# Cross-attention with layer norm: attention values in two halves per block, and a new written order of the steps on every engine

## The chip, the cores and the metric

One core of a Trainium2 chip runs the whole program. The metric is the device time of one execution in microseconds (us). Engines are called by the profile's names: PE (matmul; PEld its weight loads), DVE (vector), ACT (scalar activation), POOL (GpSimd), SP (issues the DMAs).

## The reference

Four batches of 2048 rows of `x` (512 wide) attend to 77 context rows each, with 16 heads of 32. The result passes the output projection, is added to `x` and normalised:

```python
qh = split(x @ Wq.T + bq); kh = split(ctx @ Wk.T + bk); vh = split(ctx @ Wv.T + bv)
scores = einsum('bhqd,bhkd->bhqk', qh, kh) / sqrt(32);  masked where mask == 0
e = exp(scores - max(scores)) * mask;  probs = e / (sum(e) + 1e-9)
out = einsum('bhqk,bhkd->bhqd', probs, vh) @ Wo.T + bo + x
y = (out - mean(out)) / sqrt(var(out) + 1e-5) * ln_g + ln_b
```

All arrays are float32. The kernel keeps most of that accuracy by splitting operands in a high and a low part and making three products of each.

## The kernel before

The 8192 rows of `x` are taken in 16 blocks `b` of 512 rows, four blocks to a batch. For each block the steps are:

- `Q(b, g)`: 12 matmuls of 512 columns, four times (g is a group of four heads). Before it ACT writes the high part of `xT` (`XT_hi`, two halves), POOL the low part (`XT_lo`). ACT and DVE then take the result out of the bank (`Q_hi`, `Q_lo`).
- `S(b, t, half)`: scores of 128 rows `t` and eight heads, 6 matmuls of 308 columns, eight times. DVE adds the mask bias (`bias`) and takes the maximum (`row_max`); ACT makes eight exponentials (`exponent`); after `add_eps` and `inverse`, POOL multiplies (`normalise`) and DVE transposes into TP (`turn`). There is one pair of score banks, so each `S` waits until `bias` has emptied it.
- `AV(b)`: probabilities times values, on 32x32 tiles of the array, a loop over four head groups g. It begins when all four `turn` of the block are done. `AT_hi_` (ACT) and `AT_lo_` (DVE) take it out.
- `OUT(b, i)`: 12 matmuls of 512 columns, four times. DVE runs `residual`, `stats`, `aggregate`, `center` on the bank. Then come `inv_std` (POOL), `LN_scale` (ACT), `add_beta` (POOL) and the store (SP).

`Q` and `OUT` share two PSUM banks, `qo_bank`. `QO_TURN` (L174) lists the eight units of a step, and a unit takes bank 0 or 1 by its place in this list. `qo_free` waits until the unit two places ahead has been emptied.

Nothing is scheduled at run time. Each engine has its own order written out by hand, one software-pipelined loop over steps `s` (PE L115, ACT L213, DVE L673, POOL L769, SP L295), and each instruction waits on semaphores. A step of PE holds S of block s-1, Q of block s, and AV and OUT of block s-2. PE runs, in a step, `AV(s - 2)` whole between `S(s - 1, 1, 1)` and `Q(s, 0)` (L121).

Ahead of the loop come the keys (`K`) and in its first steps the values (`V`) of all four batches. Both go through DRAM: SP stores `V_st` to V_scratch once per batch (L287), and `load_V` (L254) brings a batch back in 24 DMAs in the layout of AV; `load_K` (L240) does it for keys in 4. `V_add` (L571) on DVE writes `V_st`, which has two buffers, so the fourth waits until the second is stored. SP's order before the loop is: load_K(0), xT(1), rows(0), the V stores with load_V(0) after the first, load_K(1), load_V(1). xT(2) and all later loads come behind this.

The program text of PE reaches it by an instruction queue, q8 in the profile. Both its weight loads and its matmuls are instructions.

Of the kernel before, what the change touches and what calls it, by code (L numbers as in the profile page):

```python
# [40 lines left out]
def xattn_program(nc, xT, x, ctxT, mask, WqT, WkT, WvT, WoT, qk_b, bv, bo, ln_g, ln_b, out):  # L41
# [6 lines left out]
    with es:  # L48
# [127 lines left out]
        QO_SLOT = {(kind, i): (n, lag) for n, (kind, i, lag) in enumerate(QO_TURN)}  # L176
        assert len(QO_SLOT) == 2 * T

        def qo(kind, i):
            return qo_bank[QO_SLOT[kind, i][0] % 2]  # L180

        def qo_before(kind, b, i):
            n, lag = QO_SLOT[kind, i]
            s = b + lag
            while s >= -1:
                s, n = (s, n - 2) if n >= 2 else (s - 1, n + 2 * T - 2)
                other, j, lag = QO_TURN[n]
                if has(s - lag):
                    return other, s - lag, j
            return None  # L190
# [618 lines left out]
```

## Time and profile before

| | |
|---|---|
| median of 3 runs | 795.63 us (794.51 to 800.0) |
| profiled execution: its time | 795.72 us |
| its span, first to last instruction | 793.9 us |
| PE busy | 646.9 us (81%) |
| DVE / ACT / POOL busy | 530.6 / 529.2 / 429.7 us |
| mean granted TensorE clock | 0.872 of full |
| first AV starts / last AV starts / last instruction ends | 117.0 / 754.4 / 793.9 us |

Read it by stages: up to the first AV (117 us) is the prologue. From the second AV (158.6 us) to the fifteenth (715.6 us) the loop repeats. After that the pipeline drains. Busy shares are averages over all three. In the view of groups a matmul of full float32 counts as two instructions: an AV of one block has 192 in the program's order and 384 in the trace, with as many weight loads.

### The profile page before, as it was taken

Reading aid. Unit: us, or ns where it says so; the run is one execution under the profiler, and the core shown is the slowest. Engines: PE = TensorE matmul, PEld = TensorE weight load, DVE = VectorE, ACT = ScalarE, POOL = GpSimd, SP = SyncE. Lnnn points to the kernel's source line nnn. Section 1 sums busy time; section 2 is a strip of 40 time slices with the busy share of each in tenths; the row PEclk is TensorE's granted clock in tenths of the full one; section 3 lists DMA queues with packets and bytes.
Section 4 is the critical chain, followed back from the end, with each engine's and each line's share of the span. In section 5 each row is a group of like instructions: output and inputs, shape, how many; then the busy total and the mean of one; then the engine's idle time right before and its main releaser. Section 6 shows DMA issues by size and latency. Waiting matters only on the chain.

```text
span 793.9 us, 21417 instructions
## 1 busy us (share of the span) xinstructions
PE 646.9 (81%) x8544; PEld 529.6 (67%) x8544; DVE 530.6 (67%) x798; ACT 529.2 (67%) x2362; POOL 429.7 (54%) x332
## 2 busy tenths in 40 slices
PE   4694068989898979799898989897979899897664
PEld 4573057767676868677776767685868677676553
DVE  5445064959595967769594959586877859596733
ACT  6253275859594968669594959495968859586521
POOL 4401143557657573837574665757483747555553
PEclk9798558989897989989897989798998979896977
DMA  9703210302222031404140232203140402020202
GB/s 319 243 8 65 92 53 2 113 23 83 81 79 84 19 131 29 147 15 148 45 138 26 81 97 63 99 8 142 47 148 14 147 15 93 16 81 29 80 30 79
DMA packets 36549, 63.80 MB, mean 80 GB/s; under 512 B 12660, under 2 KB 15124, under 8 KB 34273
## 3 DMA queue, kind: packets, MB, share of 16 engines
q1 hardware_dynamic: 36304, 62.42, 24.0%
q8 instruction: 67, 1.10, 0.5%
q14 instruction: 34, 0.27, 0.1%
q10 hardware_dynamic: 144, 0.00, 0.0%
HBM read 43.43 MB, written 18.67 MB: 78 GB/s over the span
## 4 chain that ended last, share of the span: by engine, by line
PE 66%; DVE 16%; issue 10%; SPq 3%; DMA 2%; ACT 1%; POOL 1%; POOLq 0%; DVEq 0%
PE qo_bank L313 39%; PE av_bank L398 14%; PE s_bank L313 11%; DVE E L589 3%; DVE TP L617 3%; DVE qo_bank L633 3%; SPq L254 2%; DVE bn L639 2%; PE av_bank L313 2%; DVE neg_max L598 2%; DVE AT_lo L625 1%; DMA V_scratch<-V_st 1%; DMA xT_raw<-in_xT 1%; POOL xT_lo L730 1%; DMA qk_bias<-in_qk_b 1%
## 5 line engine op out<-in xcount | busy, mean ns | idle before, releaser
L482 ACT ACTIVATE E<-E,neg_max 128x77 f32<-128x77 f32 x1024 | 352.2, 350 | 15.8 <-DVE neg_max L598 15.8
L749 POOL TENSOR_TENSOR E<-E,inv_sum 128x1232 f32<-128x1232 f32 x64 | 145.7, 2277 | 209.8 <-DVE inv_sum L606 209.8
L482 ACT ACTIVATION_READ_ACCUMULATOR E<-E,neg_max 128x1 f32 x1024 | 194.6, 190 | 0.0
L398 PE MATMUL av_bank<-TP,Vp 32*32 32x128 f32 x6144 | 109.0, 326 | 52.5 <-issue 49.7
L398 PEld LDWEIGHTS av_bank<-TP,Vp 32*32 32x32 f32 x6144 | 84.8, 114 | 73.0 <-issue 63.2
L313 PE MATMUL qo_bank<-xT_hi,WqT_lo 128*128 128x512 f32 x256 | 85.3, 462 | 42.5 <-DVE QT_lo L577 35.2
L625 DVE TENSOR_TENSOR AT_lo<-av_bank,AT_hi 128x512 fp32r<-128x512 f32 x64 | 43.0, 675 | 112.9 <-ACT AT_hi L497 112.9
L589 DVE TENSOR_TENSOR E<-s_bank,mask_bias 128x616 f32<-128x616 f32 x128 | 101.0, 789 | 25.9 <-PE s_bank L313 22.8
L497 ACT ACTIVATE AT_hi<-av_bank 128x512 fp32r<-128x512 f32 x64 | 36.0, 592 | 119.7 <-PE av_bank L398 119.7
L767 POOL TENSOR_TENSOR Y<-Y,b_row 128x512 f32<-128x512 f32 x64 | 82.7, 1294 | 60.1 <-ACT Y L505 60.1
L313 PE MATMUL s_bank<-Kd,QT_hi 128*128 128x308 f32 x512 | 114.1, 310 | 0.0
L313 PE MATMUL s_bank<-Kd,QT_lo 128*128 128x308 f32 x256 | 81.8, 320 | 26.9 <-DVE E L589 24.7
L730 POOL TENSOR_TENSOR xT_lo<-xT_raw,xT_hi 128x1024 fp32r<-128x1024 f32 x32 | 77.4, 2422 | 46.0 <-ACT xT_hi L461 46.0
L598 DVE TENSOR_REDUCE neg_max<-E 128x8 f32<-128x624 f32 x128 | 100.0, 781 | 1.2
L617 DVE STREAM_TRANSPOSE TP<-E 128x1280 f32<-128x1280 f32 x64 | 95.6, 1494 | 1.0 <-POOL E L749 1.0
L577 DVE SCALAR_TENSOR_TENSOR QT_lo<-qo_bank,qk_bias,QT_hi 128x512 fp32r<-128x512 f32 x64 | 47.5, 742 | 70.9 <-ACT QT_hi L473 70.9
L313 PEld LDWEIGHTS qo_bank<-xT_hi,WqT_lo 128*128 128x128 f32 x256 | 53.0, 220 | 57.3 <-DVE QT_lo L577 35.8
L313 PEld LDWEIGHTS s_bank<-Kd,QT_hi 128*128 128x128 f32 x512 | 87.1, 194 | 4.8
L473 ACT ACTIVATE QT_hi<-qo_bank,qk_bias 128x512 fp32r<-128x512 f32 x64 | 43.7, 682 | 68.3 <-PE qo_bank L313 68.3
L313 PE MATMUL qo_bank<-WoT_lo,AT_hi 128*128 128x512 f32 x256 | 74.2, 414 | 9.7 <-DVE Y L653 8.1
L313 PE MATMUL qo_bank<-xT_lo,WqT_hi 128*128 128x512 f32 x256 | 81.7, 447 | 0.0
L741 POOL TENSOR_TENSOR Y<-Y,bo_row 128x1024 f32<-128x1024 f32 x32 | 74.6, 2353 | 3.4 <-DMA Y<-in_x 3.3
(65 smaller groups left out, 934.0 us busy)
## 6 DMA issues: line engine op xcount, KB each, us to landing
xT_raw<-in_xT SPq DMA_DIRECT2D x16, 1024.0 KB, 5.9
Y<-in_x SPq DMA_DIRECT2D x16, 1024.0 KB, 5.6
out_y<-Y SPq DMA_DIRECT2D x64, 256.0 KB, 3.7
Vp<-V_scratch SPq DMA_DIRECT2D x48, 32.0 KB
K_scratch<-TP SPq DMA_DIRECT2D x1, 1232.0 KB, 9.2
E<-in_WkT SPq DMA_DIRECT2D x4, 256.0 KB, 5.5
Y<-in_WqT SPq DMA_DIRECT2D x4, 256.0 KB, 6.6
TP<-in_WvT SPq DMA_DIRECT2D x4, 256.0 KB, 9.7
```

The lines of the kernel that those rows point to most:

```text
L313: last = mm(bank, a, b, start=(n == 0), stop=(n == len(products) - 1))
L398: last = mm(av_bank[DK * j:DK * j + DK, q, g * P:g * P + P], Vp[part, b // BB % 2, par, kb, u, :], TP[part, 5 * u + 2 * par + kb, :, :].re ...
L482: last = cp(e, e, ACT.Exp, bias=neg_max[:, t, h:h + 1], accum_out=rowsum[:, t, h:h + 1])
L577: stt(out=QT_lo[:, b % 2, g, :], in0=qo("Q", g)[:, :], scalar=qk_bias[:, g:g + 1], in1=QT_hi[:, b % 2, g, :].bitcast(FP32), op0=ALU.add, o ...
L589: tt(E[:, t, 8 * half:8 * half + 8, 0:SK].rearrange("p (g j) k -> p g j k", g=2), s_bank[:, :, 0:GK].rearrange("p g (j k) -> p g j k", j=H ...
L598: nc.vector.tensor_reduce(out=neg_max[:, t, 8 * half:8 * half + 8], in_=E[:, t, 8 * half:8 * half + 8, 0:SK + 1], op=ALU.max, axis=AX.X, n ...
L617: nc.vector.transpose(TP[:, :, t, :], E[:, t, :, :].rearrange("p h k -> p (h k)") .rearrange("p (n q) -> p n q", q=Q32)).then_inc(t_ready, 1)
L625: tt(AT_lo[:, :, cols], av_bank[:, i, :].rearrange("p (g r) -> p g r", g=C), AT_hi[:, :, cols].bitcast(FP32), ALU.subtract).then_inc(at_lo, 1)
L730: nc.gpsimd.tensor_tensor(out=xT_lo[:, b % 2, cs, :], in0=xT_raw[:, b % 2, cs, :], in1=xT_hi[:, b % 2, cs, :].bitcast(FP32), op=ALU.subtra ...
L741: nc.gpsimd.tensor_tensor(out=y, in0=y, in1=bo_row[:, :].unsqueeze(1).broadcast_to((P, 2, D)), op=ALU.add).then_inc(x_bo_ready, 1)
L749: nc.gpsimd.tensor_tensor(out=e, in0=e, in1=inv_sum[:, t, :].unsqueeze(2).broadcast_to((P, H, SK)), op=ALU.mult).then_inc(probs_ready, 1)
L767: nc.gpsimd.tensor_tensor(out=y, in0=y, in1=b_row[:, :], op=ALU.add).then_inc(normed, 1)
```

## The change

The arithmetic is the same, and so is the number of instructions of each kind on PE. What changes is order and place:

- `AV(b, pair)` has two parts, of two head groups (eight heads) each. In a step, PE now has `AV(s-2, 0)`, `S(s-1, 1, 1)`, `Q(s, 0)`, `S(s-1, 2, 0)`, `AV(s-2, 1)`. Its end is signalled after the second part only.
- `QO_ORDER` lists all 128 units of `Q` and `OUT` for the whole program, with other lists for the first and last steps, and gives each its bank in alternation. `OUT(b, 2)` and `OUT(b, 3)` stand together at the head of the next step.
- Each engine's loop has its own lists for the first and last steps. ACT takes AT_hi of all four parts together. Stores of a block go out together.
- In the prologue: the low part of the first xT is made by DVE (`XT_lo_first`) and not by POOL. The high parts of that xT come before those of the keys. `ctxT_hi/lo` lie in the second half of Kd (so this is zeroed later, in `zero_Kd_1`). load_K(1) and load_V(1) move behind xT(2) to xT(5) and rows(1), rows(2). Projections of block 0 start before the values.

```diff
-        QO_TURN = (("OUT", 3, 3), ("Q", 0, 0), ("Q", 1, 0), ("OUT", 0, 2),
-                   ("Q", 2, 0), ("OUT", 1, 2), ("Q", 3, 0), ("OUT", 2, 2))
+        QO_TURN = (("OUT", 3, 2), ("OUT", 3, 3), ("Q", 0, 0), ("Q", 0, 1), ("OUT", 2, 0), ("Q", 0, 2), ("OUT", 2, 1), ("Q", 0, 3))
...
+                    19: (("OUT", 15, 0), ("OUT", 15, 1), ("OUT", 15, 2), ("OUT", 15, 3),)}
...
+        def qo(kind, b, i):
+            return qo_bank[QO_PLACE[kind, b, i] % 2]
...
+                if b in (2, BB + 1, 2 * BB + 1):
+                    load_K(b // BB + 1)
+                    load_V(b // BB + 1)
...
-            load_K(1)
-            load_V(1)
...
-            def AV(b):
+            def AV(b, pair):
...
-                for g in range(C):
+                for g in (2 * pair, 2 * pair + 1):
...
-                last.then_inc(av_ps, 1)
+                if pair == 1:
+                    last.then_inc(av_ps, 1)
...
-                OUT(s - 3, 3), S(s - 1, 1, 1), AV(s - 2), Q(s, 0), S(s - 1, 2, 0), Q(s, 1), S(s - 1, 2, 1)
-                OUT(s - 2, 0), S(s - 1, 3, 0), Q(s, 2), S(s - 1, 3, 1), OUT(s - 2, 1)
+                    OUT(s - 3, 2), OUT(s - 3, 3), S(s - 1, 0, 1), S(s - 1, 1, 0), AV(s - 2, 0)
+                    S(s - 1, 1, 1), Q(s, 0), S(s - 1, 2, 0), AV(s - 2, 1), Q(s, 1)
+                    S(s - 1, 2, 1), OUT(s - 2, 0), S(s - 1, 3, 0), Q(s, 2), S(s - 1, 3, 1), OUT(s - 2, 1)
+                    Q(s, 3), S(s, 0, 0)
...
+            def XT_lo_first(i):
+                dve.wait_ge(xt_hi, i + 1)
+                cs = slice(2 * i, 2 * i + 2)
+                tt(xT_lo[:, 0, cs, :], xT_raw[:, 0, cs, :], xT_hi[:, 0, cs, :].bitcast(FP32), ALU.subtract) \
+                    .then_inc(xt_lo, 1)
```

Three places of the order. **PE in a step of the loop**, before. `av_bank` rows are AV, `s_bank` rows S, `qo_bank` rows with xT are Q:

```order
L313 MATMUL s_bank<-Kd,QT_lo 128x308
L313 MATMUL s_bank<-Kd,QT_hi 128x308 x2
L398 MATMUL av_bank<-TP,Vp 32x128 x192
L313 MATMUL qo_bank<-xT_hi,WqT_lo 128x512 x4
L313 MATMUL qo_bank<-xT_lo,WqT_hi 128x512 x4
L313 MATMUL qo_bank<-xT_hi,WqT_hi 128x512 x4
L313 MATMUL s_bank<-Kd,QT_lo 128x308
```

and changed:

```order
L446 MATMUL av_bank<-TP,Vp 32x128 x96
L360 MATMUL s_bank<-Kd,QT_lo 128x308
L360 MATMUL s_bank<-Kd,QT_hi 128x308 x2
...
L360 MATMUL qo_bank<-xT_hi,WqT_lo 128x512 x4
L360 MATMUL qo_bank<-xT_lo,WqT_hi 128x512 x4
L360 MATMUL qo_bank<-xT_hi,WqT_hi 128x512 x4
...
L446 MATMUL av_bank<-TP,Vp 32x128 x96
L360 MATMUL qo_bank<-xT_hi,WqT_lo 128x512 x4
```

The run of 192 became two runs of 96. Between them lie two S and one Q, 24 matmuls.

**SP at the end of the prologue**, before. The V stores come first, then Kd and Vp of batch 1, then xT (`Y<-in_x` are the rows for the residual, `out_y` is a store):

```order
L287 DMA V_scratch<-V_st 616x1x32 [waits v_ready]
L287 DMA V_scratch<-V_st 616x1x32
L240 DMA Kd<-K_scratch 32x8x77 [waits k_saved]
L240 DMA Kd<-K_scratch 32x8x77 x3
L254 DMA Vp<-V_scratch 32x256 [waits Vp_zeroed,v_saved1]
...
L208 DMA xT_raw<-in_xT 128x2048 [waits q_ps] x3
L220 DMA Y<-in_x 128x4x512 [waits wo_lo]
```

and changed:

```order
L300 DMA V_scratch<-V_st 616x1x32 [waits v_ready]
L300 DMA V_scratch<-V_st 616x1x32
L217 DMA xT_raw<-in_xT 128x2048 [waits q_ps] x2
L229 DMA Y<-in_x 128x4x512 [waits wo_lo]
L217 DMA xT_raw<-in_xT 128x2048 [waits q_ps]
L235 DMA out_y<-Y 128x512 [waits normed] x4
L217 DMA xT_raw<-in_xT 128x2048 [waits q_ps]
L229 DMA Y<-in_x 128x4x512 [waits stored0_2,stored0_3,stored0_1,stored0_0]
L250 DMA Kd<-K_scratch 32x8x77 [waits Kd_zeroed,k_saved]
```

28 DMAs moved from ahead of xT(2) to behind xT(5).

**PE at the end of the program**, with bank numbers, before:

```order
L398 MATMUL av_bank<-TP,Vp 32x128 x192
L313 MATMUL qo_bank1<-WoT_lo,AT_hi 128x512 x4
L313 MATMUL qo_bank1<-WoT_hi,AT_lo 128x512 x4
L313 MATMUL qo_bank1<-WoT_hi,AT_hi 128x512 x4
L313 MATMUL qo_bank1<-WoT_lo,AT_hi 128x512 x4
L313 MATMUL qo_bank1<-WoT_hi,AT_lo 128x512 x4
L313 MATMUL qo_bank1<-WoT_hi,AT_hi 128x512 x4
L313 MATMUL qo_bank1<-WoT_lo,AT_hi 128x512 x4
```

and changed:

```order
L446 MATMUL av_bank<-TP,Vp 32x128 x192
L360 MATMUL qo_bank0<-WoT_lo,AT_hi 128x512 x4
L360 MATMUL qo_bank0<-WoT_hi,AT_lo 128x512 x4
L360 MATMUL qo_bank0<-WoT_hi,AT_hi 128x512 x4
L360 MATMUL qo_bank1<-WoT_lo,AT_hi 128x512 x4
L360 MATMUL qo_bank1<-WoT_hi,AT_lo 128x512 x4
L360 MATMUL qo_bank1<-WoT_hi,AT_hi 128x512 x4
L360 MATMUL qo_bank0<-WoT_lo,AT_hi 128x512 x4
```

OUT(15, 0), (15, 1) and (15, 2) all used bank 1; now the banks alternate. The two parts of the last AV still stand together (192).

## Rows read from the trace of the kernel before

**Rows 1.** Windows, the loop's whole stretch: us, busy of each engine (instructions), PEclk, DMA share, GB/s

```profile
158.56:754.40 595.84, 523.52 (x7321) 430.47 (x7320) 436.49 (x664) 437.79 (x2003) 360.88 (x279) 0.89 0.23 74
```

**Rows 2.** Waits of PE from 150 us on: us in total, times, longest

```profile
PE av_bank L398 <- issue: 47.6, 31, 3.1
PE s_bank L313 <- DVE E L589: 21.9, 16, 1.8
```

**Rows 3.** Timeline of PE, AV(1) and AV(14): start, us, line, count, [idle before <-releaser]

```profile
158.56 2.72 PE L398 MATMUL av_bank<-TP,Vp 32*32 32x128 f32 x190
162.59 1.90 PE L398 MATMUL av_bank<-TP,Vp 32*32 32x128 f32 x128 [1.31 <-issue]
166.04 1.54 PE L398 MATMUL av_bank<-TP,Vp 32*32 32x128 f32 x66 [1.55 <-issue]
...
715.61 2.65 PE L398 MATMUL av_bank<-TP,Vp 32*32 32x128 f32 x183
...
723.27 1.97 PE L398 MATMUL av_bank<-TP,Vp 32*32 32x128 f32 x73 [1.11 <-issue]
```

**Rows 4.** Timeline of PE, first matmuls of an S, a Q and the next S

```profile
387.32 0.30 PE L313 MATMUL s_bank<-Kd,QT_lo 128*128 128x308 f32 x1
...
388.18 1.10 PE L313 MATMUL qo_bank<-xT_hi,WqT_lo 128*128 128x512 f32 x4
...
390.99 0.30 PE L313 MATMUL s_bank<-Kd,QT_lo 128*128 128x308 f32 x1
```

**Rows 5.** Windows of PE, before and in one AV: us, busy (matmuls), PEclk, DMA share, GB/s

```profile
368.00:369.00 1.00, 0.00 (x0) 1.00 0.93 365
...
380.00:381.00 1.00, 0.44 (x22) 0.50 0.00 0
```

**Rows 6.** The page's DMA queues, the instruction queue of PE: packets, MB, share

```profile
q8 instruction: 67, 1.10, 0.5%
```

**Rows 7.** Timeline, prologue: first Q and what it waits for

```profile
17.86 5.23 POOL L730 TENSOR_TENSOR xT_lo<-xT_raw,xT_hi 128x1024 fp32r<-128x1024 f32 x2 [7.35 <-ACT xT_hi L461]
...
23.14 2.08 PE L313 MATMUL qo_bank<-xT_hi,WqT_lo 128*128 128x512 f32 x4 [6.87 <-POOL xT_lo L730]
```

**Rows 8.** Timeline of SP's DMA issues in the prologue: start, us that they take

```profile
59.18 10.27 SPq L254 DMA_DIRECT2D Vp<-V_scratch  x24
...
76.56 2.57 SPq L240 DMA_DIRECT2D Kd<-K_scratch  x4
79.24 10.17 SPq L254 DMA_DIRECT2D Vp<-V_scratch  x24
```

**Rows 9.** The chain of waits, prologue: start, us, what

```profile
70.38 3.65 DMA V_scratch<-V_st
...
89.45 5.34 DMA xT_raw<-in_xT
```

**Rows 10.** Timeline of PE behind it: Q(1, 3) and Q(2, 0)

```profile
101.16 2.08 PE L313 MATMUL qo_bank<-xT_hi,WqT_lo 128*128 128x512 f32 x4 [31.95 <-DVE QT_lo L577]
...
125.96 1.35 PE L313 MATMUL qo_bank<-xT_hi,WqT_lo 128*128 128x512 f32 x4
```

**Rows 11.** The page's costliest groups: busy, mean ns of one | idle before, releaser

```profile
L482 ACT ACTIVATE E<-E,neg_max 128x77 f32<-128x77 f32 x1024 | 352.2, 350 | 15.8 <-DVE neg_max L598 15.8
L749 POOL TENSOR_TENSOR E<-E,inv_sum 128x1232 f32<-128x1232 f32 x64 | 145.7, 2277 | 209.8 <-DVE inv_sum L606 209.8
...
L617 DVE STREAM_TRANSPOSE TP<-E 128x1280 f32<-128x1280 f32 x64 | 95.6, 1494 | 1.0 <-POOL E L749 1.0
```

**Rows 12.** Timeline, the end: last AV, the OUTs of block 15, the last center

```profile
754.41 4.40 PE L398 MATMUL av_bank<-TP,Vp 32*32 32x128 f32 x236 [2.77 <-DVE TP L617]
...
764.81 1.76 PE L313 MATMUL qo_bank<-WoT_lo,AT_hi 128*128 128x512 f32 x4 [1.57 <-DVE AT_lo L625]
...
771.92 2.06 PE L313 MATMUL qo_bank<-WoT_lo,AT_hi 128*128 128x512 f32 x4 [2.53 <-DVE Y L653]
...
788.07 0.75 DVE L653 SCALAR_TENSOR_TENSOR Y<-qo_bank,mean_var,g_row 128x512 f32<-128x512 f32 x1
```

More of the change, by code:

```diff
@@ L172, in has @@
             return 0 <= b < NB
-        QO_TURN = (("OUT", 3, 3), ("Q", 0, 0), ("Q", 1, 0), ("OUT", 0, 2),
-                   ("Q", 2, 0), ("OUT", 1, 2), ("Q", 3, 0), ("OUT", 2, 2))
[L176 to L180, printed above, removed]
-        def qo_before(kind, b, i):
[L183 to L190, printed above, removed]
+        QO_TURN = (("OUT", 3, 2), ("OUT", 3, 3), ("Q", 0, 0), ("Q", 0, 1), ("OUT", 2, 0), ("Q", 0, 2), ("OUT", 2, 1), ("Q", 0, 3))
+        QO_EDGES = {-2: (("Q", 0, 0), ("Q", 0, 1),),
[5 rows of a table added]
+                    15: (("OUT", 12, 2), ("OUT", 12, 3), ("Q", 15, 0), ("Q", 15, 1), ("OUT", 13, 0), ("Q", 15, 2), ("OUT", 13, 1),),
+                    16: (("Q", 15, 3), ("OUT", 13, 2), ("OUT", 13, 3),),
+                    17: (("OUT", 14, 0), ("OUT", 14, 1), ("OUT", 14, 2), ("OUT", 14, 3),),
+                    18: (),
+                    19: (("OUT", 15, 0), ("OUT", 15, 1), ("OUT", 15, 2), ("OUT", 15, 3),)}
+        QO_ORDER = []
+        for s in range(-3, NB + 5):
+            turn = QO_EDGES.get(s, tuple((kind, s - lag, i) for kind, lag, i in QO_TURN))
+            QO_ORDER += [unit for unit in turn if has(unit[1])]
+        QO_PLACE = {unit: n for n, unit in enumerate(QO_ORDER)}
+        assert len(QO_ORDER) == len(QO_PLACE) == 8 * NB
+        def qo(kind, b, i):
+            return qo_bank[QO_PLACE[kind, b, i] % 2]
+        def qo_before(kind, b, i):
+            n = QO_PLACE[kind, b, i]
+            return QO_ORDER[n - 2] if n >= 2 else None
         @block.sync
@@ L207, in load_xT @@
                     sp.wait_ge(mask_ready, 1)
-                sp.dma_start(xT_raw[:, b % 2, :, :], xT[b]).then_inc(x_loaded[b % 2], 16)
+                for i in range(2 if b == 0 else 1):
+                    cs = slice(2 * i, 2 * i + 2) if b == 0 else slice(0, C)
+                    sp.dma_start(xT_raw[:, b % 2, cs, :], xT[b, :, cs, :]).then_inc(x_loaded[b % 2], 16)
             def load_rows(b):
@@ L470, in Q_hi @@
                     act.wait_ge(qk_loaded, 16)
-                if b == 1 and g == 0:
-                    act.wait_ge(v_ps, B)
-                cp(QT_hi[:, b % 2, g, :], qo("Q", g)[:, :], ACT.Identity, bias=qk_bias[:, g:g + 1]).then_inc(q_hi, 1)
+                cp(QT_hi[:, b % 2, g, :], qo("Q", b, g)[:, :], ACT.Identity, bias=qk_bias[:, g:g + 1]).then_inc(q_hi, 1)
             def exponent(b, t, half):
@@ L505, in LN_scale, with ctx_hi_ @@
                 cp(Y[:, b % 2, i, :], Y[:, b % 2, i, :], ACT.Copy, scale=rstd[:, b % 2, i:i + 1]).then_inc(scaled, 1)
-            for c in range(C):
+            def ctx_hi_(c):
                 if c == 0:
@@ L632, in residual @@
                 dve.wait_ge(x_bo_ready, 2 * b + i // 2 + 1)
-                tt(qo("OUT", i)[:, :], qo("OUT", i)[:, :], Y[:, b % 2, i, :], ALU.add).then_inc(y_ready, 1)
+                tt(qo("OUT", b, i)[:, :], qo("OUT", b, i)[:, :], Y[:, b % 2, i, :], ALU.add).then_inc(y_ready, 1)
             def stats(b, i):
@@ L658, in _, with ctx_lo_ @@
                 .then_inc(k_bias_ready, 1)
-            for c in range(C):
+            dve.wait_ge(k_bias_ready, 1)
+            def ctx_lo_(c):
                 dve.wait_ge(ctx_hi, c + 1)
@@ L714, in _ @@
             nc.gpsimd.memset(sum_eps_c[:, :], SUM_EPS).then_inc(consts_set, 1)
[L715 to L716 removed]
+            nc.gpsimd.memset(Kd[:, 0, :, :, :].bitcast(FP32), 0.0).then_inc(Kd_zeroed, 1)
             nc.gpsimd.memset(Vp[:, :, :, :, :, :], 0.0).then_inc(Vp_zeroed, 1)
@@ L723, in _, with zero_Kd_1 @@
             nc.gpsimd.memset(E[:, :, :, CLAMP + 1:KW].rearrange("p t h k -> p (t h) k"), 0.0).then_inc(E_pads, 1)
+            def zero_Kd_1():
+                pool.wait_ge(v_ps, B)
+                nc.gpsimd.memset(Kd[:, 1, :, :, :].bitcast(FP32), 0.0).then_inc(Kd_zeroed, 1)
             def XT_lo(b, i):
-                if not has(b):
+                if not has(b) or b == 0:
                     return
```

486 lines of the change are left out of this document (361 added, 125 removed), and 5 rows, old and new, of the table QO_EDGES.

## The prediction

> **What bounds the kernel now.** I read the windows of the loop first. Between the second and the fifteenth AV [rows 1] PE is busy 523.5 of 595.8 us, DVE 436.5, ACT 437.8, POOL 360.9. The stretch holds 14 periods, so DVE and ACT need about 31.2 us of each and have slack. PE sets the pace. The period follows from the starts of AV(1) and AV(14) [rows 3]: (715.61 - 158.56) / 13 = 42.85 us.
>
> Next, what such a period is made of. Q is 12 matmuls and takes 390.99 - 388.18 = 2.81 us; S takes 388.18 - 387.32 = 0.86 us [rows 4]. AV at full clock takes 2.72 / 190 = 14.3 ns per matmul of the trace, 5.5 us for 384 [rows 3]. A block is 4 Q + 4 OUT (same size) + 8 S + AV = 22.5 + 6.9 + 5.5 = 34.9 us. The waits [rows 2] add 21.9 / 16 = 1.4 us where two S stand together and the second waits for the bias, and 47.6 / 15 = 3.2 us in pauses inside AV whose releaser is only "issue". That makes 39.5. The missing 3.35 us per block are slow clock: it was 1.00 (2.4 GHz) in the S and OUT work at 368 us, and is 0.50 (1.2 GHz) at 380, behind the first pause of that block's AV [rows 5].
>
> The pauses have a pattern. The first run of an AV varies (190, 183), the second is always 128 matmuls, then comes the rest [rows 3]. 128 matmuls with their weight loads are 256 instructions. The instruction queue moved 67 packets of 1.10 MB in all [rows 6], 16.4 KB each, against 2 x 8544 instructions of PE: one packet is 256 instructions. From the second run's start to the third's is 166.04 - 162.59 = 3.45 us, while the 128 matmuls need 1.90. So I read it so: PE has one packet ahead, a new one takes about 3.5 us from the moment PE enters the one before, and AV eats a packet in 1.9. Q and OUT need about 30 us for one and never notice. An AV of 384 crosses the end of its current packet after r matmuls, and runs dry at r + 128 and r + 256: two pauses of about 1.6 us.
>
> The Trainium skill speaks against this reading (Runtime: NRT & Kernel Launch, "Instruction fetch mechanics"): it gives PE's instruction memory as 2048 instructions and calls the cost of crossing a 16 KiB boundary "mostly hidden". By that rule the split would remove no pause, and the time would be the second rival's. The rows repeat at every 128 matmuls, so I go by them.
>
> Last, prologue and end. In the prologue SP is the bound: V stores, 24 DMAs for Vp, six V stores, 4 DMAs for Kd, again 24 for Vp, and only then xT(2), which lands 5.34 us after 89.45 [rows 8, 9]. ACT's order has the copy of xT(2) ahead of Q_hi(1, 1), so PE stands idle 31.95 us before Q(1, 3), and Q(2, 0) starts at 125.96 [rows 10]. At the end OUT(15, 0) to (15, 2) share a bank and wait for each other: 771.92 - 764.81 = 7.1 us each [rows 12].
>
> **The loop.** AV becomes two runs of 192 matmuls. Between them lie two S and a Q, 24 matmuls in 4.5 us, long enough for a fetch. With r matmuls to the end of the packet where the first part starts:
> - r from 0 to 24: the first part runs dry at r + 128, the second at r + 168. Two pauses.
> - 24 to 64: the first part runs dry once; the next end falls in the second part's start and is covered. About one (a second, partial one to about 32).
> - 64 to 88: the second crossing falls in the S and Q. None, with partial pauses at both edges.
> - 88 to 128: crossing at r in the first part, at r - 88 and r + 40 in the second. One.
>
> A block has 528 matmuls, 4 x 128 + 16, so r moves on from block to block and is spread evenly: (24 x 2 + 8 x 1.5 + 32 + 10 x 0.5 + 8 x 0.5 + 40) / 128 = 1.1 pauses instead of 2. At 1.6 us they cost 1.8 instead of 3.2. The clock: I charge each pause the same share as before, 3.35 / 2 = 1.7, so 1.85. Bounds: none, since a gap of about 1 us without any matmul (368 us) between S and S left the clock at 1.00 [rows 5]; or the whole 3.35, since one pause in AV was enough. I take the middle because each pause now has dense Q or S near. The S wait stays 1.4 (S(s-1, 0, 1) and S(s-1, 1, 0) still adjoin). New period: 34.9 + 1.4 + 1.8 + 1.85 = 39.95 us. Bounds 38.1 and 41.5.
>
> Do the others keep up? Followed through one period: after AV's second part ACT makes 4 AT_hi, four groups of eight exponentials at 8 x 350 ns = 2.8 us, and two Q_hi, about 16 us; then inverse, normalise 2.28 and turn 1.49 [rows 11]. That is 20 us to the next AV's first part, which follows 30 us after the previous one's end. 10 us of slack. xT, rows and stores are issued when Q(s-1, 3) ends and used 12 us or more later. These moves I cost at nothing; the cover is that slack.
>
> **The prologue.** XT_lo of block 0 took POOL 5.23 us [rows 7]. On DVE two 1024-column subtractions cost about 1.3 each (estimate from its 1.49 for the 1280 columns of a turn [rows 11]), so the first Q starts at about 17.6 instead of 23.14. The keys' parts slip behind it and Kd is issued at 24 instead of 17.4, so S(0, 0, 0) comes near 30. xT(1) is issued at 27.7 and Q(1, 0) starts near 40. Then ACT is the thread: four groups of exponentials and two Q_hi bring DVE to V_add(0) at about 51. SP repeats its rows from there [rows 8]: stores, Vp from 54.8 to 65.1, second store (0.9 to issue and 3.65 to land), V_add(3) at 70, last store, and xT(2) at 72 directly, because 2.57 + 10.17 us of DMAs stand behind it. It lands at 77.3; ACT 2.0 and POOL about 5 bring Q(2, 0) at 83.3, not 125.96. PE finds AV(0)'s first part done already (about 75). From Q(2, 0) to AV(1): four Q and four OUT 22.5, cold clock 2.6 on the first, six S 5.2, wait 1.4, second part of AV(0) and a pause 4.5: 36.2, so AV(1) at 119.5 instead of 158.56. Gain 39. Bounds: 26, if only the 12.7 us of DMAs and the 13 us of AV and S done ahead count; 44, if ACT runs at no idle at all.
>
> The moved 28 DMAs are now issued near 135 us, behind xT(5), and S(4, 0, 0) needs them near 165: covered by a whole period. DVE stands 6 us at V_add(3) with `bias(1, 0, 0)` and `turn(0, 3)` behind it; this is inside the 75 above.
>
> **The end.** From AV(14)'s second part: ACT's four AT_hi and four groups of exponentials 14, inverse, normalise and turn 4, handoffs 1: AV(15) 19 us later (before 754.41 - 725.2 = 29.2). AV(15) and its AT parts as before, 764.81 - 754.41 = 10.4 [rows 12]; it is whole, with two pauses. The OUTs alternate banks: 4.6 cold, 3.7, 2.8, 2.8, then residual to center 2.5: 16.4, then as from 788.82 to 793.9, 5.1. Sum 50.9 against 68.7: gain 17.8. Bounds 10 and 20.
>
> **Sum against the profiled execution**, 795.7 (span 793.9 and 1.8 around it), which is the median of the runs shown. 795.7 - 39 - 13 x (42.85 - 39.95) - 17.8 = 795.7 - 39 - 37.7 - 17.8 = 701.2. I forecast **701 us**.
>
> **Rivals.**
> - *The clock holds.* For: the gap at 368 us did not lower it, and half AVs stand in dense work. Against: in every block before, the drop followed AV's first pause. Then the cold share is 0 and the period 38.1: 13 x 1.85 = 24 less, 677.
> - *The pauses are not packets but belong to AV*, or packets come later because of DMA traffic (one pause was 3.1 us [rows 2]). Then two remain and the period stays 42.85: 701 + 38 = 739.
> - *The prologue keeps its thread.* If ACT or DVE, blocked at xT(2) and V_add(3), let AV(1) come only the lower bound early: 701 + 13 = 714; with a period of 41.5 too, 735.
> - *Slower than before.* ACT now does all four AT_hi behind `exponent(s-1, 1, 1)`, and `normalise(s-1, 1)` on POOL stands behind two add_bo (2.3 us each) and two add_beta. If this closes a ring ACT, POOL, turn, AV, AT_hi, every block lasts that ring. It decides from (39 + 17.8) / 13 = 4.4 us above the old period: 47.2 us; at 49 the time is 795.7 - 56.8 + 13 x 6.15 = 819. Against it is the ring's length, 30 us by the sum above, which would need 17 us of waits more.
>
> **Chances.** Forecast 0.56 (own range 688 to 716), clock holds 0.14, pauses stay 0.13, prologue weaker 0.13, slower 0.04. Both ends of the range take in the first rival and the two at 735 to 739: 672 to 741. Faster by over 1% 0.95, within 1% 0.01, slower 0.04; 1% is about what a measurement here can tell from no change.
>
> **What would show it.** In the changed profile: runs of 128 between pauses still, but about 17 pauses on "issue" in the loop, not 31; periods near 40 us; clock drops in about as many blocks as have pauses; Q(2, 0) at 83 and AV(1) near 120; SP's xT(2) right behind the last V store; OUTs of block 15 without the 7.1 us step. It is wrong if PE's largest wait in the loop is a new one on DVE or ACT, or if pauses stand elsewhere than at packet ends.

## The result and the profile after

The changed kernel takes **698.75 us** (median of 4 runs, 692.32 to 703.17) where the kernel before takes 795.07 (median of 4, 788.19 to 800.0). The ratio is 0.8767, 95% interval 0.8662 to 0.8872; ratios and intervals here leave out slow runs, of which 703.17 is one. Forecast were 701 us, range 672 to 741.

The page of the changed kernel, its head and the instruction queue of PE:

```profile
span 694.9 us, 21418 instructions
PE 609.5 (88%) x8544; PEld 502.2 (72%) x8544; DVE 530.7 (76%) x800; ACT 526.9 (76%) x2362; POOL 423.9 (61%) x330
q8 instruction: 67, 1.10, 0.7%
```

The number of PE instructions and of packets is that of before [rows 6]. What changed is how long PE waits and at which clock it works. The waits of PE from 119 us to the end (engine, tile, line, what it waited for: us in total, times, longest):

```profile
PE av_bank L446 <- issue: 22.2, 17, 4.1
PE s_bank L360 <- DVE E L722: 16.3, 18, 1.1
PE qo_bank L360 <- issue: 4.4, 2, 2.5
...
PE s_bank L360 <- issue: 0.8, 1, 0.8
```

Before, the first row was 47.6 us in 31 pauses [rows 2]. Three pauses now fall just outside AV, where a packet ends in S or Q.

The timeline of PE (start, duration, engine, line, operation, count, and in brackets the idle time before it). AV(1), AV(2) and AV(3), then the block at 395 us, then a block with no pause, then the end:

```profile
124.74 2.74 PE L446 MATMUL av_bank<-TP,Vp 32*32 32x128 f32 x192
...
162.69 2.61 PE L446 MATMUL av_bank<-TP,Vp 32*32 32x128 f32 x176
166.91 0.45 PE L446 MATMUL av_bank<-TP,Vp 32*32 32x128 f32 x16 [1.62 <-issue]
...
200.77 2.29 PE L446 MATMUL av_bank<-TP,Vp 32*32 32x128 f32 x156
204.13 0.84 PE L446 MATMUL av_bank<-TP,Vp 32*32 32x128 f32 x36 [1.08 <-issue]
...
395.84 2.66 PE L446 MATMUL av_bank<-TP,Vp 32*32 32x128 f32 x182
402.61 0.66 PE L446 MATMUL av_bank<-TP,Vp 32*32 32x128 f32 x10 [4.11 <-issue]
...
593.79 2.74 PE L446 MATMUL av_bank<-TP,Vp 32*32 32x128 f32 x192
...
603.14 2.74 PE L446 MATMUL av_bank<-TP,Vp 32*32 32x128 f32 x192
...
631.02 2.71 PE L446 MATMUL av_bank<-TP,Vp 32*32 32x128 f32 x189
...
639.08 4.12 PE L446 MATMUL av_bank<-TP,Vp 32*32 32x128 f32 x192
...
664.53 3.26 PE L446 MATMUL av_bank<-TP,Vp 32*32 32x128 f32 x236
...
674.47 2.04 PE L360 MATMUL qo_bank<-WoT_lo,AT_hi 128*128 128x512 f32 x4 [1.57 <-DVE AT_lo L758]
678.72 1.09 PE L360 MATMUL qo_bank<-WoT_lo,AT_hi 128*128 128x512 f32 x4
```

The runs before the first pause get shorter by 20 from block to block (176, 156, 135 ...). So far the packet end moves. 528 - 4 x 128 would give 16; the trace has 508 matmuls from one of these pauses to the next where four packets of 128 would hold 512, and what fills the rest was not traced. The OUTs of block 15 follow each other after 4.25 us, not 7.1 [rows 12].

The windows of the loop of both kernels, AV(1) to AV(14) (length; busy time of PE, PEld, DVE, ACT, POOL; granted clock, DMA share, GB/s). After:

```profile
124.74:631.02 506.28, 468.91 (x6865) 388.67 (x6865) 412.41 (x626) 415.71 (x1899) 343.60 (x266) 0.99 0.27 85
```

and before:

```profile
158.56:715.61 557.05, 495.81 (x6866) 408.90 (x6865) 411.39 (x625) 415.72 (x1896) 339.95 (x262) 0.90 0.23 75
```

Both hold 13 periods: 42.85 us before, 38.94 now. PE is busy 26.9 us less for the same matmuls, with a granted clock of 0.99 and not 0.90; DVE and ACT are busy as long as before.

**The ledger of the two spans** (793.9 - 694.9 = 99.0 us):

| stretch (from start to start) | before | after | gain | forecast |
|---|---|---|---|---|
| start to AV(1) | 158.56 | 124.74 | 33.8 | 39 |
| AV(1) to AV(14) | 557.05 | 506.28 | 50.8 | 37.7 |
| AV(14) to the end | 78.3 | 63.9 | 14.4 | 17.8 |

In the middle row the waits of PE for the same two windows give the parts: pauses on "issue" 43.4 us before and 23.5 now (19.9), waits of S for the bias 17.9 and 13.6 (4.3), PE busy 26.9. Together 51.1.

### The profile page after: what moved, and what is told of

It reads as the page before. It is cut to its first block, busy times and chain, and to the rows that moved or that the text cites. A ratio compares the mean times of both kernels' runs of the same rounds, so it can differ in the third digit from the quotient of the medians.

```text
span 694.9 us, 21418 instructions
## 1 busy us (share of the span) xinstructions
PE 609.5 (88%) x8544; PEld 502.2 (72%) x8544; DVE 530.7 (76%) x800; ACT 526.9 (76%) x2362; POOL 423.9 (61%) x330
## 4 chain that ended last, share of the span: by engine, by line
PE 77%; DVE 7%; issue 5%; DMA 4%; SPq 3%; POOL 1%; ACT 1%; POOLq 0%; DVEq 0%
PE qo_bank L360 49%; PE s_bank L360 15%; PE av_bank L446 12%; DMA xT_raw<-in_xT 3%; DVE E L722 3%; SPq L264 1%; DMA V_scratch<-V_st 1%; DVE TP L750 1%; POOL E L962 1%; ACT xT_hi L537 1%; SPq L202 1%; POOL xT_lo L943 1%; DVE AT_lo L758 1%; DVE WoT_lo L684 0%; SPq L250 0%
## 5 line engine op out<-in xcount | busy, mean ns | idle before, releaser
L722 DVE TENSOR_TENSOR E<-s_bank,mask_bias 128x616 f32<-128x616 f32 x128 | 101.1, 790 | 72.8 <-PE s_bank L360 71.2
L446 PE MATMUL av_bank<-TP,Vp 32*32 32x128 f32 x6144 | 94.8, 285 | 22.2 <-issue 22.2
L360 PE MATMUL s_bank<-Kd,QT_lo 128*128 128x308 f32 x256 | 84.6, 331 | 33.2 <-DVE E L722 33.1
L943 POOL TENSOR_TENSOR xT_lo<-xT_raw,xT_hi 128x1024 fp32r<-128x1024 f32 x30 | 71.1, 2391 | 57.4 <-ACT xT_hi L537 57.4
L446 PEld LDWEIGHTS av_bank<-TP,Vp 32*32 32x32 f32 x6144 | 76.8, 104 | 37.7 <-issue 32.5
L360 PEld LDWEIGHTS s_bank<-Kd,QT_lo 128*128 128x128 f32 x256 | 49.8, 195 | 47.5 <-DVE E L722 29.6
L579 ACT ACTIVATE Y<-Y,rstd 128x512 f32<-128x512 f32 x64 | 43.9, 719 | 49.8 <-POOL rstd L972 48.6
L360 PE MATMUL qo_bank<-xT_hi,WqT_lo 128*128 128x512 f32 x256 | 74.9, 415 | 6.5 <-POOL xT_lo L943 3.8
L360 PE MATMUL qo_bank<-xT_lo,WqT_hi 128*128 128x512 f32 x256 | 72.6, 406 | 2.5 <-issue 2.5
L547 ACT ACTIVATE QT_hi<-qo_bank,qk_bias 128x512 fp32r<-128x512 f32 x64 | 43.4, 680 | 40.7 <-PE qo_bank L360 40.5
L360 PE MATMUL qo_bank<-WoT_hi,AT_lo 128*128 128x512 f32 x256 | 71.7, 402 | 0.0
L360 PE MATMUL qo_bank<-xT_hi,WqT_hi 128*128 128x512 f32 x256 | 71.3, 401 | 0.0
```

Of the source, the lines that this page charges most:

```text
L360: last = mm(bank, a, b, start=(n == 0), stop=(n == len(products) - 1))
L446: last = mm(av_bank[DK * j:DK * j + DK, q, g * P:g * P + P], Vp[part, b // BB % 2, par, kb, u, :], TP[part, 5 * u + 2 * par + kb, :, :].re ...
L547: cp(QT_hi[:, b % 2, g, :], qo("Q", b, g)[:, :], ACT.Identity, bias=qk_bias[:, g:g + 1]).then_inc(q_hi, 1)
L579: cp(Y[:, b % 2, i, :], Y[:, b % 2, i, :], ACT.Copy, scale=rstd[:, b % 2, i:i + 1]).then_inc(scaled, 1)
L722: tt(E[:, t, 8 * half:8 * half + 8, 0:SK].rearrange("p (g j) k -> p g j k", g=2), s_bank[:, :, 0:GK].rearrange("p g (j k) -> p g j k", j=H ...
L943: nc.gpsimd.tensor_tensor(out=xT_lo[:, b % 2, cs, :], in0=xT_raw[:, b % 2, cs, :], in1=xT_hi[:, b % 2, cs, :].bitcast(FP32), op=ALU.subtra ...
```

## The experiments

Three questions were left: is the split what gains in the loop, or the new order; are the pauses packets; and what makes some of them 4 us long.

**The split undone in the changed kernel.** AV runs whole where its first part stood.

```diff
-                if not has(b):
+                if not has(b) or pair == 1:
...
-                for g in (2 * pair, 2 * pair + 1):
+                for g in range(C):
```

Expected: 

> The changed kernel with AV whole again: both parts at the place of the first, every other order as in the change. Theory (packets of 256 PE instructions): two pauses on issue in every block again, the second run of each AV 128 matmuls, about 3.2 us per block instead of 1.8, and the granted clock low behind them in nearly every block. Period 42 to 43 us instead of 38.9, time 740 to 755. Rival (the gain of the loop comes from the new order of the other steps): period stays 39, time about 700.

Measured: 777.72 us (776.26 to 780.06), ratio to before 0.9758 (0.9708 to 0.9809). So the split carries 79 us of the 96 in this order, more than the 41 to 56 expected. PE's pauses from 120 us on, a wait that is new, and the loop:

```profile
PE av_bank L446 <- issue: 57.4, 31, 4.5
...
PE qo_bank L360 <- DVE AT_lo L757: 11.5, 14, 1.9
```

```profile
127.89:706.93 579.04, 502.26 (x6865) 411.80 (x6865) 409.01 (x626) 415.01 (x1899) 344.06 (x266) 0.90 0.24 75
```

31 pauses and the clock of 0.90 are back. They are longer than in the kernel before (57.4 us against 47.6; five of them last 3.6 to 4.5), and a wait for AT_lo is new; what brings it was not traced. Of the 72.8 us by which this loop is longer than that of the change, 28.0 are pauses, 33.4 PE's busy time (the clock) and 8.1 the new wait. The period is 579.04 / 13 = 44.5 us, longer than the 42.85 of before. The new order without the split is worth something only in the prologue and at the end.

**The split alone in the kernel before**, with its own order, one Q and one S between the parts.

```diff
-                OUT(s - 3, 3), S(s - 1, 1, 1), AV(s - 2), Q(s, 0), S(s - 1, 2, 0), Q(s, 1), S(s - 1, 2, 1)
+                OUT(s - 3, 3), S(s - 1, 1, 1), AV(s - 2, 0), Q(s, 0), S(s - 1, 2, 0), AV(s - 2, 1), Q(s, 1), S(s - 1, 2, 1)
```

Expected: 

> The kernel before with one edit: AV in two parts, with Q(s, 0) and S(s-1, 2, 0) between them; all other orders as before. Theory: pauses fall from 31 to about 17 in the loop and the clock holds in most blocks, so the period falls by 3 to 4 us and the time to about 745. Rival (the other engines' orders were made for a whole AV, and AT_hi, 3.7 us later on ACT, holds up the exponentials and the next AV): fewer pauses, but a new wait in their place; period above 41, time 765 to 795.

Measured: 801.61 us (795.87 to 804.37, 10 runs), ratio 1.0067 (1.0030 to 1.0103): no gain, and above the range of the rival too. Its new wait came, but for a bank and not for AT_hi. The two largest waits of PE from 120 us on, and one block (DVE Y L655 is `center`, which empties the bank of an OUT):

```profile
PE qo_bank L313 <- DVE Y L655: 38.0, 17, 2.5
PE av_bank L399 <- issue: 25.8, 17, 2.8
```

```profile
383.24 1.96 PE L399 MATMUL av_bank<-TP,Vp 32*32 32x128 f32 x134
385.49 1.01 PE L399 MATMUL av_bank<-TP,Vp 32*32 32x128 f32 x58 [0.30 <-issue]
388.79 1.33 PE L313 MATMUL qo_bank<-xT_hi,WqT_lo 128*128 128x512 f32 x4 [2.29 <-DVE Y L655]
389.91 1.91 PE L313 MATMUL qo_bank<-xT_lo,WqT_hi 128*128 128x512 f32 x4
```

The split does its work at once: pauses fall from 31 to 17. But Q(s, 1) now comes before `center` of OUT(s-3, 3) has emptied its bank. A pause of 1.6 us in AV became a wait of 2.3 us behind it, and the clock falls behind that one too (the rows after it take 1.33 and 1.91 us instead of 1.09). So the split gains only with the new order: OUT and Q in another order, with the bank table made for it. Which part of that order frees the bank in time was not tried by itself.

**V(3) computed four times**, 36 more matmuls ahead of the loop. It moves every packet end against AV and changes nothing else in the loop.

```diff
-                    ... Q(1, 3), V(2), V(3)
+                    ... Q(1, 3), V(2), V(3, True), V(3, True), V(3, True), V(3)
```

Expected: 

> The changed kernel with V(3) computed four times instead of once in the prologue (36 more matmuls of PE, while it is idle there anyway). Theory of packets: every later pause moves by 36 matmuls: the first part of AV(2), which ran dry after 176, runs dry after 140; AV(3) after 120 instead of 156; AV(4) after 99 instead of 135; AV(1), which had none, after 160. Time within 1% of the change. Rival (the pauses belong to AV, a DMA or a wait): the same run lengths as in the change.

One run, 722.74 us. The first runs of AV(1), AV(2) and AV(3) were 160, 140 and 120 matmuls, where the changed kernel has 192, 176 and 156. The last two are shorter by exactly 36; in AV(1) of the changed kernel the pause stood 4 matmuls behind the 192, in the S that follows. AV(4), expected to stop after 99, had no pause in its first part: its packet is entered 29 larger matmuls ahead of the part, which leaves time for the next one. So a count of instructions, not a place in AV, sets the pauses. The time was a miss: 24 us more, not within 1%. It was run again, four times.

Expected: 

> The changed kernel with V(3) computed four times, 36 extra matmuls ahead of the loop, timed in rounds this time. If the one run of 722.7 us was typical, the median is 715 to 728 and the ends of the packets against the transfers cost 3 to 4 per cent. If that run was an outlier, the median lies within 1% of the change's 698.8.

Measured: 715.51 us (714.02 to 717.38), ratio 0.9016 (0.8988 to 0.9044). The first part of its AV(1), the second part of its AV(3), and the windows around the pause in the latter:

```profile
123.69 2.32 PE L447 MATMUL av_bank<-TP,Vp 32*32 32x128 f32 x160
...
216.15 2.30 PE L447 MATMUL av_bank<-TP,Vp 32*32 32x128 f32 x159
221.53 0.56 PE L447 MATMUL av_bank<-TP,Vp 32*32 32x128 f32 x33 [3.08 <-issue]
222.02 1.66 PE L360 MATMUL qo_bank<-xT_hi,WqT_lo 128*128 128x512 f32 x4
```

```profile
215.00:218.40 3.40, 3.40 (x167) 2.86 (x166) 2.14 (x3) 3.40 (x16) 2.16 (x1) 1.00 0.58 214
218.40:221.50 3.10, 0.05 (x4) 0.00 (x0) 0.02 (x1) 0.77 (x5) 1.12 (x1) 1.00 0.30 111
221.50:226.00 4.50, 4.47 (x43) 3.38 (x43) 3.28 (x4) 2.06 (x4) 4.50 (x3) 0.62 0.01 4
```

These windows are of the pause at 218.4 to 221.5 us. The DMA engines moved 214 GB/s in the 3.4 us ahead of it, the pause was 3.08 us, and the clock was 0.62 in the 4.5 us behind it. SP had issued the rows of x at 214.78.

**The rows of x not loaded.** The same kernel with the shift, and the changed kernel without it, load 2 of 128 partitions of x for blocks 2 to 15 (the result of those blocks is then wrong; the instructions are the same).

```diff
-                sp.dma_start(Y[:, b % 2, :, :], x_rows[b]).then_inc(rows_in[b % 2], 16)
+                n = P if b < 2 else 2
+                sp.dma_start(Y[0:n, b % 2, :, :], x_rows[b][0:n]).then_inc(rows_in[b % 2], 16)
```

Expected of the one with the shift: 

> The same shift of 36 matmuls, but the load of the rows of x for blocks 2 to 15 brings 2 of 128 partitions (the output of those blocks is not the reference's; all instructions are the same, and the transfer of 1 MB that begins in every block between the two halves of the attention values is gone). Theory of traffic (a fetch of instructions that runs beside a burst of transfers takes longer): the pauses of 3 us and more at 219.9, 332.9, 375.9 and 574.1 us of the run with the shift fall to 1 to 2 us; four times 2.7 us, and the slow clock behind each (about 1 to 2 us), make it 13 to 18 us shorter than the kernel with the shift: about 707 us where that one takes 722. The long pause near 176 us beside the loads of K and V stays. Theory of place (the pause is long for where it stands in the values, whatever the transfers do): the long pauses stay, and the time within 1% of the kernel with the shift.

Expected of the one without: 

> The changed kernel without the shift, with the same small loads of x for blocks 2 to 15 (the output of those blocks is not the reference's). Theory of traffic: only the pause of 4.11 us at 402.6 us and perhaps that of 2.49 lay beside such a load, so 3 to 7 us with the clock behind them: 692 to 696 us where the change takes 698.8. Theory of place: within 2 us of the change.

Measured: 689.48 us (686.06 to 689.79) with the shift and 686.68 (681.54 to 692.82) without; ratios 0.8673 (0.8639 to 0.8708) and 0.8630 (0.8588 to 0.8672). The AV that answers to the one above:

```profile
214.56 0.56 PE L448 MATMUL av_bank<-TP,Vp 32*32 32x128 f32 x33 [1.19 <-issue]
```

and PE's pauses in AV in the same kernel, from 119 us on:

```profile
PE av_bank L448 <- issue: 18.9, 15, 1.9
```

The runs of AV are the same, 159 and 33, and 3.08 us became 1.19, at full clock: the first rows of Q behind it take 1.20 and 1.09 us instead of 1.66 and 1.91. The longest pause fell from 5.0 to 1.9 us. Without the load the shift costs 2.8 us, inside the runs' spread; with it, 16.8. **The theory of traffic holds**: 26 us less with the shift (13 to 18 expected) and 12 without (3 to 7 expected; here the two intervals just touch). Both were expected too small; with the shift because the long pause near 174 us, put down to the loads of K and V, went as well: the load of rows stands right ahead of those (169.78 in the timed run) and was in it. It is also seen without these runs: of the 15 pauses over 2.6 us in the changed kernel, in the one with the shift (both runs) and in the unsplit one, none had a DMA share below 0.28 in the pause itself; with a share under 0.01 none was longer than 2.45, and that one had 0.79 in the 3.4 us ahead of it. The other way round it does not hold: the pause at 242.39 in the changed kernel had a share of 0.99 and lasted 1.06.

How a load slows a fetch is in the traces, since they hold PE's instruction packets (q8) one by one. Take the pause of 4.11 us in the changed kernel, 398.50 to 402.61. PE enters its last packet at about 396.6 (128 matmuls ahead of the next one's start). The first line is the data queue q1 from then to 400.20 (packets, MB, share of the 16 DMA engines), where q8 has no line; the second is q8 from 400.20 to 401.35:

```profile
q1 hardware_dynamic: 501, 1.01, 95.3%
...
q8 instruction: 1, 0.02, 5.7%
```

Until 400.20 the 16 DMA engines are 95% busy with data. Then the packet begins, at 400.29; it takes 1.05 us, and PE resumes 1.27 us behind its end. Without such a load, as in the second pause of AV(1) before [rows 3], the packet begins 1.1 us after PE enters the one ahead, takes 1.0, and PE resumes 1.4 behind it: the 3.45 us of the prediction. In all 263 pauses on "issue" behind 60 us of the 13 traces PE resumes 1.2 to 1.6 us behind the end of a packet, and the packet takes 0.9 to 1.7. In the 24 pauses over 2.6 us it takes no longer (0.9 to 1.4), but it begins 2.3 to 4.3 us after PE enters the one ahead. In the pause at 218.45 above it is 2.6 us, and without the rows of x 0.8. So the pauses are waits for packets, and a load of data delays the start of a packet, not its transfer.

**K and V of batch 1 loaded ahead of xT(2)**, as before the change, with the zeroing of Kd's second half moved ahead on POOL.

```diff
-                if b in (2, BB + 1, 2 * BB + 1):
+                if b in (BB + 1, 2 * BB + 1):
...
+            load_K(1)
+            load_V(1)
```

Expected: 

> The changed kernel with the 28 DMAs of load_K(1) and load_V(1) back ahead of xT(2) (zero_Kd_1 moved ahead on POOL, where POOL is idle). Theory (SP's order sets when xT(2) comes and ACT is blocked on it): xT(2) is issued about 12.7 us later, near 90, AV(1) starts at about 137 instead of 124.7, time about 711. Rival (the V chain through V_add(3) sets it): no change, 699.

One run, 723.62 us. The row of SP's queue that answers to 77.55 of the change:

```profile
90.50 0.84 SPq L217 DMA_DIRECT2D xT_raw<-in_xT  x2
```

xT(2) is issued at 90.50 instead of 77.55, and AV(1) starts at 139.96 instead of 124.74: 15.2 us. AV(1) was expected at about 137. This part of the prologue's gain is shown. Another 11 us come from the loop, with 39.8 us per period; that was not expected. The pauses there stand at the same matmuls as in the change. They are 2.3 us longer in sum (one of 2.49 us is 4.52), and PE's busy time is 8.6 us longer, at a clock of 0.97 and not 0.99. The four runs of the change lie 11 us apart themselves, so one run does not show a cause.

**One bank for OUT(15, 0) to (15, 2).**

```diff
+        QO_BANK = {unit: n % 2 for unit, n in QO_PLACE.items()}
+        QO_BANK["OUT", 15, 1] = QO_BANK["OUT", 15, 0]
```

Expected: 

> The changed kernel with OUT(15, 0), (15, 1), (15, 2) in one PSUM bank, as before. Theory: (15, 1) and (15, 2) each wait for the center of the one ahead, steps of 5.4 us or more (7.1 where the clock falls) instead of 2.8; from the first OUT of block 15 to the end 26 to 29 us instead of 20.4, time about 706. Rival (the end is set by the stores): no change.

One run, 712.04 us. Its OUTs of block 15:

```profile
680.11 2.05 PE L364 MATMUL qo_bank<-WoT_lo,AT_hi 128*128 128x512 f32 x4 [1.58 <-DVE AT_lo L762]
688.10 1.21 PE L364 MATMUL qo_bank<-WoT_lo,AT_hi 128*128 128x512 f32 x4 [2.53 <-DVE Y L790]
695.23 1.44 PE L364 MATMUL qo_bank<-WoT_lo,AT_hi 128*128 128x512 f32 x4 [2.53 <-DVE Y L790]
```

Steps of 8.0 and 7.1 us are back, and from the first OUT to the end it is 30.2 us instead of 20.4 (26 to 29 expected). The banks are worth 9.8 us of the gain at the end. Of the 15.4 by which it exceeds the profiled run of the change, 4.7 lie ahead of AV(15), where nothing was edited, and 0.9 in AV(15).

**AV in four parts**, as what the packets suggest: 96 matmuls eat less than a packet, and between them PE has 6 to 18 larger ones.

```diff
-                    OUT(s - 3, 2), OUT(s - 3, 3), S(s - 1, 0, 1), S(s - 1, 1, 0), AV(s - 2, 0)
-                    S(s - 1, 1, 1), Q(s, 0), S(s - 1, 2, 0), AV(s - 2, 1), Q(s, 1)
+                    OUT(s - 3, 2), OUT(s - 3, 3), S(s - 1, 0, 1), AVq(s - 2, 0), S(s - 1, 1, 0), AVq(s - 2, 1)
+                    S(s - 1, 1, 1), Q(s, 0), AVq(s - 2, 2), S(s - 1, 2, 0), AVq(s - 2, 3), Q(s, 1)
```

Expected: 

> The changed kernel with AV in four parts in the loop's general steps: S(s-1,0,1), part, S(s-1,1,0), part, S(s-1,1,1), Q(s,0), part, S(s-1,2,0), part, Q(s,1). Theory: a part is 96 matmuls, less than a packet, and an S between adds 0.86 us, so a packet lasts 2.6 us instead of 1.9 against a fetch of 3.5: pauses of at most 0.9, and the 0.9 us wait between the two S goes under AV. Period about 37.3 instead of 38.9, time 680 to 685. Rival (each switch between AV and the rest costs about 0.2 to 0.3 us, and TP is not ready earlier): no gain, 697 to 703.

Measured: **670.92 us** (669.52 to 673.38), ratio 0.8429 (0.8388 to 0.8470), below the 680 to 685 expected. Its waits of PE from AV(1) to AV(14):

```profile
PE s_bank L360 <- DVE E L724: 5.9, 6, 1.5
PE av_bank L448 <- issue: 3.1, 9, 0.7
```

Pauses are nearly gone, and so are most waits of S: a quarter of AV now stands between S(s-1, 0, 1) and S(s-1, 1, 0), which adjoined before. The period is (603.80 - 124.93) / 13 = 36.8 us, and the granted clock 1.00.

**xT(2) ahead of the V stores**, issued behind the rows of block 0.

Expected: 

> The changed kernel with xT(2) issued before SP waits for the values. Theory: ACT no longer stands 17 us at the copy of xT(2); the exponentials of block 1 start 6 us earlier, bound then by V_add(3) at 75 us; AV(1) at 118 instead of 124.7, time about 692. Rival: the V chain alone sets it, no change.

Measured: 690.63 us (687.93 to 695.3), ratio 0.8679 (0.8625 to 0.8734). AV(1) starts at 116.53, 8.2 us earlier; the time is 8.1 less, though the two intervals overlap.

**Both.**

Expected: 

> Both edits (AV in four parts, xT(2) early). If the gains add: about 675. If the quarters give nothing: 692.

Measured: **665.56 us** (659.93 to 668.73), ratio 0.8372 (0.8318 to 0.8425), the fastest median of all, below the 675 expected (its interval still overlaps that of the four parts alone). AV(1) starts at 117.06, and its loop has this row:

```profile
117.06:595.40 478.34, 468.70 (x6865) 381.89 (x6864) 411.62 (x626) 413.79 (x1899) 344.36 (x266) 1.00 0.29 90
```

PE is busy for 98% of that stretch at full clock; another order could gain 9.6 us there at most.

## Why the prediction was right

The total was met within 3 us, and the mechanism was the one forecast. That the total is so close is in part luck: against the profiled run (696.7 us, 4.5 below the 701.2) the loop gained 13.1 us more than forecast, and prologue and end 5.2 and 3.4 less.

- **Pauses per block: right in sum.** Forecast were 1.1 per block of 1.6 us, so 1.8 us. The loop has 17 pauses on "issue" in 13 periods, 23.5 / 13 = 1.81 us: 1.3 per block of 1.4 us, two errors that cancel. A pause of 4.11 us beside a load is among them, for which the sum had no term; one rival named DMA traffic. The reading as packets of 128 matmuls was forecast with its rows and is now shown by the shift of 36 and by the q8 packets themselves. The Trainium skill (Runtime: NRT & Kernel Launch, "Instruction fetch mechanics") says of a block of 256 instructions that the sequencer's own DMA queue fetches it; the size and the queue agree with these runs. Its "mostly hidden" does not hold here: with the matmuls only moved, 20 us of pauses went from the loop.
- **Clock: the step that was mis-sized.** "I charge each pause the same share as before, 3.35 / 2 = 1.7, so 1.85" kept 1.85 us of slow clock per block and so gained 19.5 over 13. PE's busy time fell by 26.9, and what is left of slow clock is 0.7 us per block (below). The granted clock of the loop is 0.99. Four stretches show what is left:

```profile
363.00:366.00 3.00, 3.00 (x10) 2.43 (x9) 0.53 (x1) 0.96 (x3) 3.00 (x2) 0.57 0.03 5
401.00:407.00 6.00, 4.39 (x21) 3.57 (x22) 1.82 (x5) 2.48 (x12) 1.24 (x3) 0.50 0.01 3
489.00:493.00 4.00, 3.76 (x19) 2.88 (x19) 3.18 (x4) 2.06 (x4) 4.00 (x4) 0.59 0.00 0
636.00:650.00 14.00, 12.60 (x218) 9.98 (x217) 8.68 (x12) 11.37 (x53) 9.42 (x6) 0.52 0.35 110
```

  The forecast "clock drops in about as many blocks as have pauses" was wrong. In the loop it fell to 0.50 (1.2 GHz) at three pauses of 17: 2.45 us (to 362.8), 4.11 (to 402.6) and 1.20 (to 489.2). It stayed at 1.00 behind those of 1.62 at 165.3 and 2.49 at 441.0. For the clock the rival "the clock holds" was closer, though its total of 677 us was not; its 38.1 us per block lies below the measured 38.94.
- **Waits of S and the work: small misses.** The waits were left at 1.4 us per block and are 13.6 / 13 = 1.05. The work itself is more than 34.9. The pause-free block takes 631.02 - 593.79 = 37.23 us, of which 1.8 are two waits of S: 35.4. The half us more stands next to AV and behind waits: the S after AV's first part takes 597.57 - 596.46 = 1.11 us and the one ahead of the second part 0.94, where 0.86 was reckoned. So: 35.4 + 1.05 + 1.81 + what is left of the 38.94, 0.7 of slow clock. On the same base the kernel before had 42.85 - 35.4 - 17.9 / 13 - 43.4 / 13 = 2.7 us of slow clock per block, where the prediction had 3.35.
- **Prologue: 33.8, not 39.** The first Q came at 17.35 (17.6 forecast). Three steps failed. "V_add(0) at about 51" was 54.65, since the exponentials of block 0 and Q_hi(1, 1) hold ACT until 53.1. "xT(2) at 72" was 77.55. And Q(2, 0) came 15.2 us behind that and not 11.3. SP's queue (SPq: the issue of DMAs, with their count), then DVE and PE, from 60 us on:

```profile
60.55 9.95 SPq L264 DMA_DIRECT2D Vp<-V_scratch  x24
70.55 6.96 SPq L300 DMA_DIRECT2D V_scratch<-V_st  x6
77.55 1.03 SPq L217 DMA_DIRECT2D xT_raw<-in_xT  x2
```

```profile
75.11 0.69 DVE L698 TENSOR_TENSOR V_st<-av_bank,bv_row 77x512 f32<-77x512 f32 x1 [8.21 <-DMA V_scratch<-V_st]
...
85.82 4.25 DVE L684 TENSOR_TENSOR WoT_lo<-Y,WoT_hi 128x512 fp32r<-128x512 f32 x2 [1.62 <-ACT WoT_hi L519]
...
90.84 0.62 PE L360 MATMUL s_bank<-Kd,QT_lo 128*128 128x308 f32 x1 [4.99 <-DVE E L722]
```

  The first V_add came 3.6 us later than forecast and its store took 2.1 us longer to land; from there to xT(2) the steps were as reckoned. That xT(2) stands behind the stores for no need is what the early load shows: 8 us. Then xT_lo was ready at 89.52, but PE's order has an S ahead of Q(2, 0), and the bias that frees its bank stood behind the low parts of Wo (`WoT_lo`) on DVE until 90.0; the sum had put these at nothing. Q(2, 0) started at 92.75 instead of 83.3, and from there to AV(1) it was 32.0 us instead of 36.2.
- **End: 14.4, not 17.8.** The 17.8 were reckoned from the end of AV(14)'s second part (643.2): it is 694.9 - 643.2 = 51.7 us, where 50.9 was forecast. AV(15) came 21.3 us after it and not 19, with OUTs of block 14 in front, one of them held 2.39 us until `center` had emptied its bank; from the first OUT of block 15 to the end it was 20.4 and not 21.5. What the sum left out is AV(14) itself. In two parts, with S between, it lasts 643.2 - 631.02 = 12.2 us instead of 9.6, its second part at the low clock (4.12 us for 192 matmuls, 2.74 at 603).
- **Slower than before**: no sign of a ring. No wait of PE in the loop is on ACT or POOL.

## What to carry to other kernels

Runs of many tiny matmuls use up instructions faster than they are fetched: look for pauses on "issue" at a fixed count, and put large matmuls between pieces shorter than that count. Pieces of three quarters of a packet did better here than pieces of one and a half. The split alone lost all its gain at the next bank that was not yet empty, so its order has to come with it. And DMAs in front of a load that starts a long chain cost 8 us (V stores) and 15 (K and V).

## What was not expected of the hardware

- **An instruction packet that falls due during a load starts late.** The load of 1 MB of rows made pauses of 3 to 5 us, and without it the longest was 1.9; behind the one shown above PE worked 4.5 us at a clock of 0.62. The packet itself takes about 1 us in both cases. The Trainium skill (DMA: Bandwidth & Descriptors, "Issuing engines are not separate DMA queues") says of DMAs from different engines that they run on the same 16 DMA engines. That instruction packets do too is in line with these runs: one begins when the engines' share for data falls from 95% to 9%. Where the two meet they do not show.
- **The place of packet ends is a property of the whole program.** 36 matmuls in the prologue cost 16.8 us (2.4%), most of it in the loop; without the loads of x, 2.8, which is within the runs' spread. So a kernel with the same loop but other code ahead of it can differ by some per cent. The surplus in the loop of the run with K and V early is not this: its packets end at the same matmuls.
- **The clock stayed up behind most single gaps.** Before, it fell in the loop in every block, behind the first pause of its AV or at the second, with 128 small matmuls between them. After, with large matmuls close by, 14 pauses of 17 left it at 1.00. That one block has fewer pauses, and that the matmuls around them are larger, was not told apart.
